# A two-block macaron layer on one core: the experts' results fetched in two parts, and several queues reordered

## The chip, the cores and the metric

One core of one Trainium2 chip runs the whole program. The metric is the device time of one execution in microseconds (us). Engines are named as in the profile: PE (TensorE), DVE (VectorE), ACT (ScalarE), POOL (GpSimd), SP (the engine that only issues DMAs here).

## The reference

`x` is (8, 256, 128) in float32, 2048 tokens of 128 numbers. Three steps follow one another:

```python
x = x + 0.5 * ffn(layernorm(x))     # first feed-forward block
x = x + attention(layernorm(x))     # 16 heads of 8 numbers, 256 keys, rotary embedding
x = x + 0.5 * ffn(layernorm(x))     # second feed-forward block, same weights

def ffn(x):
    shared = (silu(x @ sg.T) * (x @ su.T)) @ sd.T          # hidden size 256
    logits = x @ gate_w.T                                  # 8 experts
    top = argmax(logits); xs = x * sigmoid(max(logits))
    routed = (silu(xs @ wg[top].T) * (xs @ wu[top].T)) @ wd[top].T
    return shared + routed
```

## The kernel before, in words

The tokens lie in `x` as 16 tiles of 128 (a tile has one token on each partition); four tiles are a chunk, two tiles are a batch of attention. Every engine runs its own written-out queue, and semaphores order them. The work has five stages.

**First front** (`ffn(0)` up to `routed`). DVE takes moments of each chunk, POOL turns the variances into inverse deviations (`ffn_rstd`), DVE normalises, PE transposes (`turn_chunk`) and multiplies with the gate (`logits`). DVE chooses an expert for each token (`choose`), PE counts tokens by expert (`count`), DVE works out each token's slot (`place`). This is done in two steps: tiles 0 to 11 (`FIRST = 12`), then 12 to 15. ACT scales the tokens (`scale`), and POOL scatters them by slot into `xs_sorted` in DRAM, one indirect DMA a tile (L323). Between these, PE does the shared expert chunk by chunk: `shared_gate`, `shared_up`, `shared_down`; ACT applies SiLU (`silu`), DVE multiplies (`shared_hidden`) and adds to `x` (`shared_add`). `find_experts` tells PE which expert each slot tile has; PE loads these 23 numbers into registers.

**Routed experts** (`routed`). 23 slot tiles (`SLOT_TILES`) are loaded back (`LOADS`, on SP), and each goes through its expert: PE transposes, gate and up products, SiLU on ACT, product on DVE, transposes, down product. POOL scatters each result tile to its tokens' rows in `y_by_token` (L332). The scatter of tokens is such that the tokens of tiles 0 to 11 are all in slot tiles 0 to 18.

**Return.** SP waits for all 23 result scatters (`y_scattered`), then loads the results in four pieces of a chunk into `yg`, which lies in the same memory as `xs`. DVE adds half of them to `x` (`add_experts`, L782).

**Attention** (`attention(turn)`, turns i = -3 to 8). A turn has 16 steps n on each engine. PE computes scores of batch i twice: in one orientation for the row maxima (`scores`, DVE `maxima`, L801), which run 12 steps ahead, and in the other for the exponentials (`scores_t`, ACT `exponentials`, L535). Around them are the later batches' normalisation, projections (`project`), rotary embedding (`rope` on DVE, `rotate`, `remainder`, `third` on POOL, `first` and `second` on ACT), and the transposes `turn_parts` of queries and keys in halves (qa, ka, qb, kb) and of the halves with the maxima's parts in them (ma, mb). POOL's `split_max` makes these parts from the eight maxima of a half. The copies out of PSUM are `copy_queries` and `copy_keys`. Turns -3 to -1 are the prologue. The last two turns hold parts of the second block's front.

**Second front, routed experts, return** (`ffn(1)`): as before, then SP stores `x` to `out_x` in four pieces, each after its `add_experts`.

## Time and profile before

| | |
|---|---|
| Three runs | 351.35, 354.33 and 354.4 us, median 354.33 |
| The profiled execution | 352.44 us, of which the span from first to last instruction is 350.6 |
| Mean granted clock of PE | 0.953 |
| Busy shares | PE 82%, DVE 66%, ACT 57%, POOL 46% |
| The chain that ended last, by engine | PE 50%, DVE 27%, DMA 6%, issue 6%, POOL 5%, ACT 4% |
| Stages in the span | first front to 49.4, routed experts to about 89, return and prologue of attention to about 124, attention to about 270, second front to 297.8, routed experts to 337.5, return and stores to 350.6 |

Times within the span are microseconds from its start. The busy shares are averages over stages with different limits, so they are to be read by stage. The 1.84 us outside the span are start and end of the execution.

### The profile page before, as it was taken

To read this page: it belongs to the slowest core of one execution; us is meant where nothing else is said; L and a number is where in the kernel's file an instruction comes from. 1 tells how busy PE (TensorE), PEld (TensorE's weight loads), DVE (VectorE), ACT (ScalarE), POOL (GpSimd) and SP (SyncE) were. 2 spreads that over 40 slices of the span, in tenths; PEclk is the share of its full clock that TensorE was granted. 3 is DMA by queue.
4 is the path that set the end of the run, shared out by engine and by line. 5 is a ranking of instruction groups with operands and counts; after the bars stand their busy time and mean duration, and the time that the engine had idled before them with its cause. 6 is when DMAs were issued, how large, how long until landed. Compare 5 with 4: busy or idle time off the path is not lost.

```text
span 350.6 us, 6524 instructions
## 1 busy us (share of the span) xinstructions
PE 287.1 (82%) x2124; PEld 181.0 (52%) x2146; DVE 232.0 (66%) x633; ACT 198.6 (57%) x440; POOL 161.1 (46%) x295
## 2 busy tenths in 40 slices
PE   0799959999145579999999999998999897999940
PEld 0765536666013235565656555555485565566630
DVE  6648814343165988898989899997966686334323
ACT  1254215454214578989898989897857531455410
POOL 2405788766334635253535264541210675256550
PEclk9999999999755999999999999999998999999995
DMA  7992136111310000000000000000000013511118
GB/s 205 169 328 94 53 91 132 53 47 37 107 43 0 2 0 4 0 3 2 0 2 3 0 3 2 2 1 3 2 0 3 23 55 85 142 47 37 39 46 239
DMA packets 24272, 18.42 MB, mean 53 GB/s; under 512 B 4944, under 2 KB 22608, under 8 KB 23984
## 3 DMA queue, kind: packets, MB, share of 16 engines
q1 hardware_dynamic: 21744, 12.88, 14.9%
q0 software_dynamic: 2496, 5.13, 4.5%
q8 instruction: 18, 0.29, 0.4%
q14 instruction: 14, 0.11, 0.1%
HBM read 10.30 MB, written 7.71 MB: 51 GB/s over the span
## 4 chain that ended last, share of the span: by engine, by line
PE 50%; DVE 27%; DMA 6%; issue 6%; POOL 5%; ACT 4%; SPq 1%; POOLq 0%; another core or an unknown queue 0%; DVEq 0%; ACTq 0%
PE bank L931 40%; DVE negmax L801 11%; PE bank L1098 3%; DVE qT L794 3%; PE bank L1060 3%; DVE xn L612 2%; DMA xs<-y_by_token 2%; DVE rs L818 1%; PE bank L1046 1%; PE bank L940 1%; DMA y_by_token<-ys,xg 1%; DMA x<-in_x 1%; DVE stats L622 1%; ACT kT L542 1%; DVE sh L719 1%
## 5 line engine op out<-in xcount | busy, mean ns | idle before, releaser
L801 DVE TENSOR_REDUCE negmax<-bank 128x2 f32<-128x512 f32 x128 | 83.5, 682 | 5.7 <-PE bank L931 4.1
L535 ACT ACTIVATE probs<-bank 128x512 f32<-128x512 f32 x128 | 71.8, 603 | 16.2 <-PE bank L931 15.8
L332 POOL DMA_INDIRECT y_by_token<-ys,xg x46 | 44.7, 972 | 32.5 <-issue 22.9
L766 DVE TENSOR_TENSOR rh<-rsg,bank 128x256 f32<-128x256 f32 x46 | 19.4, 421 | 47.5 <-ACT rsg L513 47.5
L931 PE MATMUL bank<-qT,kT 128*128 128x256 bf16 x256 | 49.1, 276 | 1.7 <-ACT qT L551 0.7
L323 POOL DMA_INDIRECT xs_sorted<-xs,slot x32 | 32.2, 1006 | 39.5 <-ACT xs L467 16.4
L931 PE MATMUL bank<-rgu,xgT 128*128 x92 | 47.2, 596 | 0.7 <-ACT xgT L505 0.7
L931 PE MATMUL bank<-kT,qT 128*128 128x512 bf16 x106 | 40.3, 380 | 5.0 <-DVE negmax L801 3.6
L513 ACT ACTIVATE rsg<-bank 128x256 f32<-128x256 f32 x46 | 17.7, 385 | 36.9 <-PE bank L931 36.9
L931 PE MATMUL bank<-probs,vx 128*32 128x256 f32 x512 | 35.0, 393 | 0.0
L542 ACT COPY kT<-bank 64x1024 bf16<-64x1024 bf16 x32 | 32.1, 1004 | 5.0 <-PE bank L1098 4.2
L1098 PE MATMUL bank<-tabb,parts 128*128 128x128 bf16 x384 | 30.1, 223 | 4.4 <-POOL parts L365 2.2
L931 PE MATMUL bank<-xnT,shgu 128*128 128x512 f32 x64 | 32.3, 635 | 0.5 <-DVE x L869 0.5
L1098 PEld LDWEIGHTS bank<-tabb,parts 128*128 128x128 bf16 x384 | 24.9, 100 | 13.6 <-POOL parts L365 8.2
L931 PEld LDWEIGHTS bank<-qT,kT 128*128 128x128 bf16 x256 | 21.0, 98 | 18.7 <-issue 8.3
L376 POOL TENSOR_TENSOR rot<-rc,rs 128x256 f32<-128x256 f32 x16 | 11.6, 725 | 38.7 <-DVE rs L818 38.7
L931 PE MATMUL bank<-rdn,rhT 128*128 x184 | 28.3, 277 | 0.1
L563 ACT CAST parts<-rot 128x384 bf16<-128x384 f32 x32 | 14.7, 507 | 19.3 <-POOL rot L376 16.3
L931 PEld LDWEIGHTS bank<-rdn,rhT 128*128 128x128 f32 x184 | 24.2, 191 | 0.5 <-issue 0.5
L362 POOL CAST parts<-negmax 128x16 bf16<-128x16 f32 x16 | 4.2, 260 | 38.8 <-DVE negmax L801 38.8
L931 PEld LDWEIGHTS bank<-probs,vx 128*32 128x32 f32 x512 | 13.5, 110 | 15.9 <-issue 5.5
L505 ACT COPY xgT<-bank 128x128 f32<-128x128 f32 x46 | 11.8, 260 | 15.1 <-PE bank L1046 15.1
(114 smaller groups left out, 493.2 us busy)
## 6 DMA issues: line engine op xcount, KB each, us to landing
rgu<-in_rgu SPq DMA_DIRECT2D x1, 2048.0 KB, 20.1
xs<-y_by_token SPq DMA_DIRECT2D x8, 256.0 KB, 3.6
xg<-xs_sorted SPq DMA_DIRECT2D x6, 258.0 KB, 4.4
xs_sorted<-xg SPq DMA_DIRECT2D x1, 1483.5 KB, 16.2
x<-in_x SPq DMA_DIRECT2D x4, 256.0 KB, 4.8
rdn<-in_rdn SPq DMA_DIRECT2D x1, 1024.0 KB, 16.2
out_x<-x SPq DMA_DIRECT2D x4, 256.0 KB, 2.6
xg<-xs_sorted SPq DMA_DIRECT2D x4, 193.5 KB, 3.7
```

What stands on the lines that cost most here:

```text
L323: g.indirect_dma_start(xs_dram, bass.IndirectOffsetOnAxis(ap=slot[:, i:i + 1], axis=0), xs[:, i, :], None, bounds_check=SLOT_TILES * P - 1 ...
L332: g.indirect_dma_start(y_dram, bass.IndirectOffsetOnAxis(ap=xg[:, j, D:ROW].bitcast(U32), axis=0), ys[:, j, :], None, bounds_check=N + SLO ...
L376: g.tensor_tensor(rot[:, t, :], rc[:, t, :], rs[:, t, :], ALU.add).then_inc(rotated, 1)
L505: a.copy(xgT[:, j % 2, :], gT_bank[j % 2][:, 0:P]).then_inc(gT_copied, 1)
L513: a.activation(rsg[:, 1 - u, :], gu_bank[1 - u][:, 0:F], ACT.Silu).then_inc(rsilu, 1)
L535: a.activation(probs[:, h % 8, :], stbank[st_bank(i, h)][:], ACT.Exp, scale=float(DH) ** -0.5).then_inc(exp_done, 1)
L542: ins = a.copy(kT[v][64 * k:64 * k + 64, 4 * half:4 * half + 4, k, :], src[64 * k:64 * k + 64])
L563: ins = a.copy(dst, part_of.unsqueeze(2).to_broadcast([P, H, rows, DH]))
L766: v_.tensor_tensor(rh[:, 1 - u, :], rsg[:, 1 - u, :], gu_bank[1 - u][:, F:2 * F], ALU.mult).then_inc(rh_ready, 1)
L801: v_.tensor_reduce(negmax[:, w, t, h0 + 2 * pair:h0 + 2 * pair + 2], sbank[k % 2][:].rearrange("p (a s) -> p a s", a=2), AX.X, ALU.max, ne ...
L931: return t_.matmul(o_, l, r, start=start, stop=stop, **k)
L1098: ins = t_.transpose(to[:, at:at + P], parts[w][:, t, q, h:h + 2, :].rearrange("p a c -> p (a c)"), identb)
```

## The change

1. **Layout in DRAM.** `x_in`, `y_by_token` and `out_x` are held partition by partition (the row of token (p, i) is p*16 + i), so that a partition's part of a load or store is one run of 1 or 2 KB instead of runs of 512 B. What lies in on-chip memory is the same.
2. **Return in two parts.** The results of tiles 0 to 11 are fetched once slot tiles 0 to 18 are scattered (`HOME = 19`), the rest after the last. There are six pieces (`PIECES`): tiles 0-1, 2-3, 4-7, 8-11, 12-13, 14-15. In the first block pieces 0 and 1 are added in turn -3, the others one by one at n = 13 of turns -2 to 1. The stores of `out_x` have the same pieces. All of SP's loads of results stand ahead of its stores in its queue.
3. **Slot tiles.** The first load of slot tiles (0-4) is split into 0-1 and 2-4.
4. **Queues of the fronts.** `count(0)` goes between the two halves of `shared_gate(0)`, ahead of `turn_chunk(3)`. Up products go ahead of down products. In the second block, gate and up of chunk 0 move from n = 6 and 10 of turn 8 to n = 4 and 6, and the logits of chunks 0 to 2 from n = 8, 8, 9 of turn 7 to 8, 10, 11. `count(1, 0)` goes from n = 15 to 14.
5. **Prologue of attention.** POOL's `inverse_std` of turn -2 goes ahead of `rotate`. In turn -1 the second projection with its `rope` goes behind the first two scores, and the transposes and copies of qb, kb and ma go to n = 11, the keys' copies staying at n = 9 of ACT's queue.
6. **ACT.** The SiLU table is loaded by a dummy activation at the top of turn 8; four tiles are scaled ahead of the first SiLU of the first block.
7. **`find_experts`** has one multiplication over 1x552 less.

```diff
-LOADS = [(0, SURE), (SURE, 8), (8, 12), (12, 16), (16, 20), (20, SLOT_TILES)]
+LOADS = [(0, 2), (2, SURE), (SURE, 8), (8, 12), (12, 16), (16, 20), (20, SLOT_TILES)]
+HOME = FIRST + E - 1
+PIECES = [(0, 2), (2, 4), (4, 8), (8, FIRST), (FIRST, 14), (14, TILES)]
...
-            xv = x_in.rearrange("(c i p) d -> c p i d", p=P, i=CHUNK)
+            xv = x_in.rearrange("p (c i d) -> c p i d", i=CHUNK, d=D)
...
-                sp.wait_ge(y_scattered, 16 * SLOT_TILES * (n + 1))
-                yv = y_dram[0:N, :].rearrange("(c i p) d -> c p i d", p=P, i=CHUNK)
-                for c in range(CHUNKS):
-                    sp.dma_start(yg[:, c * CHUNK:(c + 1) * CHUNK, :], yv[c]).then_inc(y_loaded[c], 16)
-            ov = out.rearrange("(c i p) d -> c p i d", p=P, i=CHUNK)
-            for c in range(CHUNKS):
-
-                sp.wait_ge(ffn_added, TILES + (c + 1) * CHUNK)
-                sp.dma_start(ov[c], x[:, c * CHUNK:(c + 1) * CHUNK, :]).then_inc(out_stored, 16)
+                yv = y_dram[0:N, :].rearrange("(p i) d -> p i d", i=TILES)
+                for k, (i0, i1) in enumerate(PIECES):
+
+                    if i0 == 0:
+                        sp.wait_ge(y_scattered[0], 16 * HOME * (n + 1))
+                    if i0 == FIRST:
+                        sp.wait_ge(y_scattered[1], 16 * (SLOT_TILES - HOME) * (n + 1))
+                    sp.dma_start(yg[:, i0:i1, :], yv[:, i0:i1, :]).then_inc(y_loaded[k], 16)
+            ov = out.rearrange("p (i d) -> p i d", d=D)
+            for i0, i1 in PIECES:
+
+                sp.wait_ge(ffn_added, TILES + i1)
+                sp.dma_start(ov[:, i0:i1, :], x[:, i0:i1, :]).then_inc(out_stored, 16)
...
+                if i == -2:
+                    inverse_std()
                 if T.pr:
                     rotate(0)
...
-                if T.nx:
+                if T.nx and i != -2:
                     inverse_std()
...
                     tanh(n, 0)
+                    scale(n, 0, range(HELD))
                     silu(0)
                     copy_chunk(n, CHUNKS - 1)
-                    scale(n, 0, range(FIRST))
+                    scale(n, 0, range(HELD, FIRST))
...
-                    if n == 13 and T.m:
+                    if n == (10 if i == -1 else 13) and T.m:
                         copy_queries("ma")
...
                     if i == B and n == 0:
+                        a.activation(table_use[:, 2:3], neghalf[:, 0:1], ACT.Silu)
                         scale(1, 0, range(HELD))
...
                 if i == -3:
+
+                    add_experts(0, 0)
                     moments_of(3, v)
+                    add_experts(0, 1)
...
+                    if n == 13 and -2 <= i <= 1:
+
+                        add_experts(0, i + 4)
...
-                    if n == 3 and T.pr:
+                    if n == (5 if i == -1 else 3) and T.pr:
                         rope(1)
...
-                    if n == 7 and T.m:
+                    if n == (11 if i == -1 else 7) and T.m:
                         copy_queries("qb")
...
-                    shared_gate(n, 0)
+                    shared_gate(n, 0, [0])
+                    count(n, 0)
+                    shared_gate(n, 0, [1])
+                    shared_up(n, 0)
                     turn_chunk(n, 3)
-                    count(n, 0)
-                    shared_up(n, 0)
                     logits(n, 3)
                     shared_gate(n, 1)
+                    shared_up(n, 1)
                     shared_down(n, 0)
-                    shared_up(n, 1)
...
-                    if i == B - 1 and n == 8:
-                        logits(1, 0)
-                        logits(1, 1)
-                    if i == B - 1 and n == 9:
-                        logits(1, 2)
-                    if i == B - 1 and n == 15:
+                    if i == B - 1 and n in (8, 10, 11):
+                        logits(1, (8, 10, 11).index(n))
+                    if i == B - 1 and n == 14:
                         count(1, 0)
-                    if i == B and n == 6:
+                    if i == B and n == 4:
 
                         pe.wait_ge(exp_done, H * B)
                         shared_gate(1, 0)
-                    if i == B and n == 10:
+                    if i == B and n == 6:
                         pe.wait_ge(pv_copied, B)
                         shared_up(1, 0)
...
-                    if n == 3 and T.pr:
+                    if n == (1 if i == -1 else 3) and T.pr:
                         project(0)
...
-                    if n == 3 and T.pr:
+                    if n == (5 if i == -1 else 3) and T.pr:
                         project(1)
...
-                    if n == 7 and T.m:
+                    if n == (11 if i == -1 else 7) and T.m:
                         turn_parts("qb")
-                    if n == 8 and T.m:
+                    if n == (11 if i == -1 else 8) and T.m:
                         turn_parts("kb")
...
-                    if n == 14 and T.m:
+                    if n == (11 if i == -1 else 14) and T.m:
                         pe.wait_ge(m_split, 2 * (i + 1) + 1)
                         turn_parts("ma")
```

## Rows read from the trace of the kernel before

**Rows 1.** Windows: length, busy (count) by engine, PEclk, DMA share, GB/s.

```profile
...
100.00:110.00 10.00, 4.44 (x15) 2.32 (x16) 6.92 (x24) 3.19 (x8) 5.33 (x11) 0.50 0.00 0
...
280.00:300.00 20.00, 17.83 (x96) 11.73 (x95) 13.04 (x35) 4.79 (x13) 11.85 (x13) 1.00 0.32 86
...
```

**Rows 2.** Chain of work that ended last, first front: start, us.

```profile
...
43.28 2.29 DMA xs_sorted<-xs,slot
45.58 3.71 DMA xg<-xs_sorted
...
```

**Rows 3.** Timeline, first front: start, us, operation, [idle before, releaser].

```profile
...
7.10 0.88 DVE L622 BATCH_NORM_STATS2 stats<-x 128x6 f32<-128x128 f32 x4 [1.54 <-DMA x<-in_x]
...
18.27 3.76 PE L931 MATMUL bank<-xnT,shgu 128*128 128x512 f32 x4
...
19.91 0.21 DVE L654 CAST onehotb<-onehot 128x96 bf16<-128x96 f32 x1
...
22.68 1.13 PE L931 MATMUL bank<-onehotb,tabb 128*128 128x96 bf16 x13
...
23.84 0.43 DVE L675 TENSOR_TENSOR over<-bank,tab 128x256 f32<-128x256 f32 x1 [3.63 <-PE bank L931]
...
45.00 2.02 PE L931 MATMUL bank<-shdn,sh 128*128 128x128 f32 x16 [1.57 <-DVE sh L719]
...
49.43 0.41 PE L1046 MATMUL bank<-tab,xg 128*128 128x128 f32 x2 [2.41 <-DMA xg<-xs_sorted]
...
```

**Rows 4.** Windows of half a microsecond in the opening loads.

```profile
...
3.00:3.50 0.50, 0.00 (x0) 0.00 (x0) 0.50 (x1) 0.00 (x0) 0.00 (x0) 1.00 0.92 335
...
8.00:8.50 0.50, 0.00 (x0) 0.00 (x0) 0.49 (x5) 0.00 (x0) 0.02 (x1) 1.00 1.07 360
...
```

**Rows 5.** Timeline, 76 to 122: first boundary, prologue of attention.

```profile
...
84.92 0.97 POOL L332 DMA_INDIRECT y_by_token<-ys,xg  x1 [0.66 <-issue]
...
90.61 0.97 POOL L332 DMA_INDIRECT y_by_token<-ys,xg  x1 [0.30 <-issue]
...
95.77 0.69 DVE L782 SCALAR_TENSOR_TENSOR x<-xs,x 128x512 f32<-128x512 f32 x1 [6.67 <-DMA xs<-y_by_token]
...
105.34 0.71 POOL L407 TENSOR_TENSOR rstd<-rstd,neghalf 128x2 f32<-128x2 f32 x1
...
109.15 1.89 PE L1098 MATMUL bank<-tabb,parts 128*128 128x128 bf16 x16 [0.95 <-POOL parts L389]
...
113.15 0.91 PE L931 MATMUL bank<-wqkv,xnT 128*128 128x384 f32 x2 [0.54 <-ACT kT L542]
...
117.91 2.03 ACT L542 COPY kT<-bank 64x1024 bf16<-64x1024 bf16 x2 [1.22 <-PE bank L1098]
118.03 1.87 DVE L801 TENSOR_REDUCE negmax<-bank 128x2 f32<-128x512 f32 x3
...
```

**Rows 6.** Timeline, 119.8 to 142: the first maxima turned.

```profile
...
122.37 0.62 PE L1098 MATMUL bank<-tabb,parts 128*128 128x128 bf16 x8 [0.32 <-POOL parts L365]
...
```

**Rows 7.** Timeline of DVE alone, 141 to 160: steady attention.

```profile
...
146.25 0.43 DVE L816 TENSOR_TENSOR rc<-bank,tab 128x256 f32<-128x256 f32 x1 [1.00 <-PE bank L931]
...
```

**Rows 8.** Windows of 2 us in the last turns.

```profile
...
264.00:266.00 2.00, 2.00 (x17) 0.94 (x10) 0.98 (x4) 0.29 (x1) 0.00 (x0) 0.50 0.05 12
...
```

**Rows 9.** Timeline, 245 to 301: from attention to the second front.

```profile
...
272.90 1.28 ACT L477 ACT_TABLE_LOAD   x1
...
275.95 1.98 PE L931 MATMUL bank<-xnT,shgu 128*128 128x512 f32 x4 [0.52 <-DVE x L869]
...
```

**Rows 10.** The page: DMA issues, KB each, us to landing.

```profile
...
xs<-y_by_token SPq DMA_DIRECT2D x8, 256.0 KB, 3.6
...
out_x<-x SPq DMA_DIRECT2D x4, 256.0 KB, 2.6
...
```

**Rows 11.** Timeline, 331 to 351: the tail.

```profile
...
341.29 2.01 SPq L292 DMA_DIRECT2D xs<-y_by_token  x4
...
346.19 1.46 DVE L782 SCALAR_TENSOR_TENSOR x<-xs,x 128x512 f32<-128x512 f32 x2 [0.30 <-DMA xs<-y_by_token]
...
```

66 lines of the change are left out of this document (29 added, 37 removed).

## The prediction

> **What bounds the kernel now.** I read the windows first, to cut the span into stages, then the chain of waits within each, and the timeline at each border. In the first front PE works almost without pause up to its last down product at 45.00, which ends at 47.02; then it waits 2.41 us for the first slot tiles [rows 3]. That load hangs on the twelfth token scatter, which takes 2.29 us to land, and on the load's own 3.71 us [rows 2]. So two paths end 2.4 us apart: POOL's scatters last, PE's shared expert next. The routed stage is a steady turn on PE which the change leaves alone. At the first border all engines stop: the last result scatter is issued at 90.61 and DVE's first addition starts at 95.77, after 6.67 us idle [rows 5]. In the prologue that follows each engine waits for another, and PE is granted 0.50 of its clock, the 1.2 GHz level, with 4.44 us of work in 10 [rows 1]. From the first turned maxima, at 122.37 [rows 6], to about 270 attention is balanced: DVE, PE and ACT each work over nine tenths of the time. The second front is PE's: 17.83 of 20 us busy [rows 1]. In the tail nothing but DMA and four additions is left: the loads of results are issued from 341.29, the last addition ends at 347.65 [rows 11], and a store takes 2.6 us more [rows 10].
>
> **First front: 2.3 us (1.0 to 3.3).** The count of tiles 0 to 11 needs the one-hot table, ready at 20.12 (19.91 + 0.21), but runs at 22.68, behind the whole first gate product and a transposition; DVE's placing starts at 23.84 [rows 3]. Half a gate product (half of 3.76) fills PE until 20.15. The count then takes its 1.13, or up to 1.5 since early matmuls are slow (the gate's four take 3.76 here and 1.98 in the second front [rows 3, 9]), so placing starts near 21.6: 2.2 us earlier. The first load becomes two tiles instead of five, which I take as 0.9 of its 3.71. The scatter path thus gains 3 us and is no longer last. What is late next is PE: its 2.41 us of waiting are the most it can give, less what the new order costs it. Here the fourth chunk's transposition stands directly ahead of its logits, and PE must wait for ACT's copy between them, about 0.6 us; the wait for the hidden product that it had before the first down product (0.5 us) goes. The 1.57 us before the last down product [rows 3] stay, since PE loads the expert numbers there. With the slow matmuls shifted a little I get PE's end 0.6 later than 47.02, so 1.8 us gained by this edit. The removed multiplication in `find_experts` and ACT's four early scalings lie beside PE's work and count for nothing; if that cover went, they would cost 0.7 and 1.3.
>
> The new layout of `x` can move the start of everything: DVE waits 1.54 us for chunk 1 [rows 3], which is its bound. The nearest rows say how much longer runs bring: with 512 B runs alone on the queues the engines moved 335 GB/s at a share of 0.92, with weights in long runs 360 at 1.07 [rows 4]. The half megabyte ahead of and in chunk 1 would come 0.1 to 0.3 us sooner by that; fewer descriptors may also fill the dip between the first loads. I take 0.5 of 0 to 1.4. The Trainium skill (DMA: Bandwidth & Descriptors, Specifications) gives 512 B as the smallest transfer at line rate; by that rule the longer runs bring nothing and the front's sum would be 1.8. Rows 4 nearly agree.
>
> **First border and prologue: 4.5 us (3.0 to 6.5).** The nineteenth scatter is issued at 84.92 [rows 5]. Landing like those of [rows 2] it is home by 87.2; a load of results lands after 2.8 to 3.6 us [rows 10], so batch 0 is there at about 90.0, when DVE has just ended its last copy. POOL cannot take the variance before its last scatter is out, 90.61 + 0.97 = 91.6. Before, it began after the addition (0.69) and the moments (about 0.9), near 97.4. So the chain starts 5.7 us earlier. The POOL step moved ahead of `rotate` in turn -2 took 105.34 + 0.71 back to 105.03, 1.0 us between the second rotation and the remainder [rows 5]; ACT's part of that tile hides 0.2 of it, so 0.8 more: the first transposition of queries, 109.15 before, comes 6.5 earlier.
>
> Then turn -1 gives some of it back. The second projection (0.91 at 113.15 [rows 5]) behind two scores lets the maxima start 8 us earlier than before in all, but its `rope` (1.0) then stands among them. The eighth maximum ends 7.4 earlier, and so do the maxima's parts. But qb and kb are now transposed only after the eighth scores. The keys' two copies on ACT take 2.03 [rows 5] and start when kb is there; scores 9 wait for them, and DVE, which had those copies long done before, stands idle for 1.7 us (its queries' copy fills the rest). The addition of piece 3 (0.69, row of 95.77) and the `rope` also count. From first to thirteenth maximum DVE took 9.8 us; I get 9.8 + 1.0 + 1.7 + 0.7 = 13.2 (a maximum is 0.6, from three in 1.87 [rows 5]). So 8.0 - 3.4 = 4.6 at the top of turn 0. ACT's second parts stand behind the copy of ma; POOL's third parts end 2.6 us later against the maxima, and PE waits for them with the next queries: I get 5.6 gained there, so DVE's stream decides. The low end takes the queries' delay in full twice; the high end has the maxima's parts (7.4) decide less 0.9 for DVE.
>
> **Turns 0 and 1: -0.2 (0 to -0.8).** Two additions of half size, 0.4 each, enter DVE's steady stream. DVE idles 1.00 us a turn at its projections [rows 7], which hides most of them.
>
> **Turn 7: +1.0 (0 to 1.6).** PE is the bound here: 2.00 busy of 2.00, at granted 0.50 in 264 to 266 [rows 8], right behind a block of 24 logits products of 8 columns. Spread over n = 8, 10, 11 the logits no longer stand in a block, and I expect no fall; PE's roughly 3 us at half rate in and beside that window would come back as half of it, less what isn't PE's.
>
> **Turn 8: -0.4 (-1.0 to +0.3).** The gate product fills PE's 0.8 us wait for ACT's copy. But the SiLU table's 1.28 [rows 9], hidden nowhere before the first SiLU, now stands ahead of that copy, and up stands ahead of the back transposition of the outputs instead of behind: PE then waits for DVE's copy (0.4) before the output product, and 0.5 after it as before [rows 9]. I get gate(1) at 276.4 instead of 275.95. Earlier counting moves the scatters, not PE.
>
> **Second front: 0 (-0.5 to +0.5).** The products are the same and PE is the bound; the reordering of up and down moves waits which sum to 0.5 either way.
>
> **Tail: 2.5 us (1.5 to 3.3).** Three quarters of the results are loaded and added while the last four slot tiles run, since 19 tiles are scattered some 6 us before the end. After the last scatter lands (341.28) two small loads are issued, landing near 344.3; two additions of 0.4 end at 345.0; the last store lands 2.6 later, 347.6. Before it was 347.65 + 2.6 = 350.2. The first four stores wait in SP's queue behind those loads, so they are issued from 342.2 on, and 0.77 MB at about 300 GB/s end near 346.3, ahead of the last. The low end lets this transfer push the last store by 1 us. A second effect of the early loads, that they share engines with the last four scatters, is hidden as long as those land before 341.3; POOL's 0.30 us gaps between them say they are issue-bound.
>
> **The sum.** 2.3 + 4.5 - 0.2 + 1.0 - 0.4 + 0 + 2.5 = 9.7 us off the profiled 352.44 (span 350.6 and 1.84 around it): 342.7. The median of the runs shown, 354.33, is 1.9 above the profiled execution. I name 343.5, between 342.7 and the 344.6 that the same step gives from the median.
>
> **The rivals.** *The clock falls in turn 7 all the same* (chance 0.25): the +1.0 is lost, 344.5. The Trainium skill (TensorE: Matmul & The Clock Gate, Why this matters for your kernels) has the throughput drop after idle gaps of PE; in rows 8 PE was not idle, so by that rule the order of logits would change nothing here. *The prologue keeps its gain* (0.15): the maxima's stream catches up in turn 0, since DVE has pauses there, and 6.5 of it remain: 341.5. *The reordered prologue gives most of it back* (0.2): keys' copies and second parts are late, PE waits in turn 0 for queries and again for keys, each of 2 us; then the border brings 2, and 346. It speaks for this that the sum of new waits on ACT's queue is 3.3 us; against it, that DVE's stream holds them once only. *The parts don't come home early* (0.04): the first loads wait in SP's queue or collide with the scatters, so that both borders stand as before; then 350. *Slower* (0.04): PE's clock, at 0.50 in the prologue [rows 1], does not come back at its end, because PE now stands still there between the eighth scores and ma and again before the queries. A steady turn at that level costs 5 us or more on PE, which is busy nine tenths at 2.4 GHz; from the second such turn on the gain of 9.7 is gone, and with three it is 358. My own forecast holds 0.32.
>
> **How the numbers follow.** The bounds of the terms reach from 351 to 337 if all fall one way, which they won't; the first three cases with theirs give 339 to 349.5. About 1% (3.5 us) is what a measurement of this kernel can tell from no change. Slower by more holds 0.03, within 1% 0.06, and the rest is faster.
>
> **What would show it.** In the new profile the routed stage starts near 47; DVE idles under 1 us at the first border, and POOL's first variance stands at its last scatter plus 0.1. In turn -1 DVE stands still before the ninth maximum. PEclk has no half-speed slice at turn 7. The last store lands about 6.3 us after the last scatter. A first border that still has DVE idle for 5 us, or more than 177 us from that first addition to the end of attention (now 174, from 95.77 to about 270), would make the prediction wrong.

## The result and the profile after

The changed kernel took 343.97 us (median of four runs, 342.91 to 344.98) where the kernel before took 354.2 (351.35 to 354.4, four runs): the ratio is 0.973, with a 95% interval of 0.967 to 0.979. The profiled execution took 343.49 us, with a span of 341.6, 9.0 less than the 350.6 before. On a second chip, where both were profiled again, it was 344.40 against 354.22, a ratio of 0.973 (0.967 to 0.979).

The rows that answer to those of before stand here in the order of the stages. First the page's line of the span and the timeline of the first front (start and length in us, engine, line, operation, idle time before it and what ended that).

```profile
span 341.6 us, 6561 instructions
...
21.86 0.42 DVE L683 TENSOR_TENSOR over<-bank,tab 128x256 f32<-128x256 f32 x1 [1.11 <-PE bank L940]
...
43.50 2.02 PE L940 MATMUL bank<-shdn,sh 128*128 128x128 f32 x16 [0.88 <-DVE x L733]
...
46.69 0.41 PE L1056 MATMUL bank<-tab,xg 128*128 128x128 f32 x2 [1.16 <-DMA xg<-xs_sorted]
```

Placing starts at 21.86 instead of 23.84, the last down product at 43.50 instead of 45.00, and the routed stage at 46.69 instead of 49.43 [rows 3]. PE still waits for the slot tiles, 1.16 us instead of 2.41. Next the first border and the prologue.

```profile
84.43 7.85 SPq L296 DMA_DIRECT2D xs<-y_by_token  x6
...
87.05 0.42 DVE L789 SCALAR_TENSOR_TENSOR x<-xs,x 128x256 f32<-128x256 f32 x1 [0.69 <-DMA xs<-y_by_token]
...
87.86 0.97 POOL L336 DMA_INDIRECT y_by_token<-ys,xg  x1 [0.30 <-issue]
...
88.84 0.28 POOL L410 TENSOR_SCALAR rstd<-meanvar 128x2 f32<-128x2 f32 x1
...
100.12 1.89 PE L1108 MATMUL bank<-tabb,parts 128*128 128x128 bf16 x16 [2.01 <-POOL parts L393]
...
112.81 0.62 PE L1108 MATMUL bank<-tabb,parts 128*128 128x128 bf16 x8 [2.24 <-POOL parts L369]
...
113.68 1.29 DVE L807 TENSOR_REDUCE negmax<-bank 128x2 f32<-128x512 f32 x2 [1.63 <-PE bank L940]
```

SP's loads start before the last scatter, and DVE's first addition waits 0.69 us instead of 6.67 [rows 5]. POOL takes the variance 0.01 us after the end of its last scatter. The queries' transposition stands at 100.12 instead of 109.15 [rows 5], the first turned maxima at 112.81 instead of 122.37 [rows 6]. DVE stands still for 1.63 us before the ninth maximum. Then windows of 2 us: the end of the prologue, and turn 7.

```profile
112.00:114.00 2.00, 1.05 (x10) 0.56 (x10) 0.37 (x2) 1.17 (x2) 0.61 (x3) 0.96 0.00 0
114.00:116.00 2.00, 1.57 (x6) 0.93 (x6) 2.00 (x4) 1.70 (x5) 0.83 (x2) 0.50 0.00 0
...
118.00:120.00 2.00, 2.00 (x14) 1.49 (x13) 1.36 (x3) 0.75 (x2) 0.00 (x0) 0.50 0.00 0
```

```profile
256.00:258.00 2.00, 2.00 (x27) 1.39 (x27) 0.17 (x1) 0.61 (x2) 0.00 (x0) 1.00 0.00 0
...
264.00:266.00 2.00, 1.85 (x8) 0.81 (x8) 1.08 (x5) 2.00 (x7) 0.00 (x0) 1.00 0.00 0
```

The granted clock (the last number but two) is at 0.96 while PE does only 1.05 us of work in 2, and is 0.50, the 1.2 GHz level, for the next 6 us, when PE works again. In turn 7 it stays at 1.00, where before it was 0.50 [rows 8]. Last the tail.

```profile
329.35 6.39 SPq L296 DMA_DIRECT2D xs<-y_by_token  x6
...
332.04 1.05 POOL L336 DMA_INDIRECT y_by_token<-ys,xg  x1 [0.30 <-issue]
...
334.70 0.69 DVE L789 SCALAR_TENSOR_TENSOR x<-xs,x 128x512 f32<-128x512 f32 x1 [0.23 <-DMA xs<-y_by_token]
335.78 3.47 SPq L301 DMA_DIRECT2D out_x<-x  x6
337.39 0.43 DVE L789 SCALAR_TENSOR_TENSOR x<-xs,x 128x256 f32<-128x256 f32 x1 [1.99 <-DMA xs<-y_by_token]
338.46 0.43 DVE L789 SCALAR_TENSOR_TENSOR x<-xs,x 128x256 f32<-128x256 f32 x1 [0.65 <-DMA xs<-y_by_token]
```

Four of six additions are done by 335.4; the last ends at 338.89 instead of 347.65 [rows 11].

**The time by stage.** Five rows of a timeline cut each span: the first transposition of a slot tile, the last result scatter of the first block, the first transposition of queries, the end of the last value product, and the same first two of the second block. This is the table of every profiled execution that follows below (us):

```
                 first  routed  border to  attention to  second  routed  tail   span
                 front          queries    last values   front
before           49.43  41.18   18.54      160.73        28.00   41.16   11.56  350.6
after            46.69  41.17   12.26      163.23        27.55   41.14    9.56  341.6
before_again     48.00  42.51   18.63      161.68        28.03   41.15   11.80  351.8
after_again      46.39  41.18   12.27      163.68        27.49   41.14    9.65  341.8
up_down_old      46.02  41.18   12.26      163.29        27.56   41.15   10.64  342.1
logits_old       46.81  41.19   12.28      163.52        27.52   41.15   11.23  343.7
x_rows_512       62.38  41.19   12.26      164.32        36.89   41.56    9.80  368.4
busy_pe          62.86  41.22   12.26      162.96        35.20   41.15   10.15  365.8
one_return       63.75  41.16   17.40      163.97        36.88   41.15   12.69  377.0
one_return_2     64.16  41.68   17.45      163.83        36.88   41.47   12.73  378.2
count_late       65.50  41.31   12.26      164.48        36.91   41.55   10.09  372.1
plain_turn       63.69  42.15   12.26      162.42        35.14   41.15   10.89  367.7
plain_turn_2     64.23  41.15   12.25      162.97        35.21   41.15   10.44  367.4
best_try         62.52  41.29   12.27      161.50        35.12   41.15   10.05  363.9
```

Between the two kernels the differences are much the same on both chips where both were profiled: +2.75 and +2.94 us up to the last scatter, +6.28 and +6.36 at the border, -2.50 and -2.00 in attention, +0.45 and +0.54 in the second front, +2.00 and +2.15 in the tail. The last eight rows come from chips on which both fronts take longer; that is told under the experiments.

Two of these sums hold different things in the two pairs. In the second, 1.33 of the 2.94 us is the first routed stage, which takes 42.51 us in before_again: the granted clock is 0.50 there from 48.3 to 51.7 us, as it isn't in before or in either profile of the changed kernel. And attention comes apart when it is cut at the ends of the value products of each batch. The five batches from the third to the seventh together take 90.0 us in all fourteen profiles; the rest is this (us):

```
                 queries to end  second   last
                 of first batch  batch    batch
before           38.06           18.35    14.32
before_again     40.38           18.35    12.96
after            41.02           18.81    13.40
after_again      41.45           18.82    13.39
up_down_old      41.09           18.81    13.40
logits_old       41.73           18.82    12.96
x_rows_512       42.12           18.80    13.40
busy_pe          40.76           18.82    13.39
one_return       41.76           18.82    13.39
one_return_2     41.63           18.81    13.39
count_late       42.26           18.82    13.39
plain_turn       40.19           18.82    13.39
plain_turn_2     40.74           18.81    13.40
best_try         39.76           18.35    13.40
```

Between kernels with the same steps the second and the last column repeat to 0.02 us (but for the 14.32, which holds the half-speed window of [rows 8]), so small effects can be read from them. The first column moves by up to 2.3 us between two profiles of one kernel; before, with 38.06, has the clock at 0.50 for 20 us up to 113.0, and before_again, with 40.38, for 27 and then 3.

### The profile page after: what moved, and what is told of

The parts are those of the page before. It is cut to its first block, busy times and chain, and to the rows that moved or that the text cites. A ratio compares the mean times of both kernels' runs of the same rounds, so it can differ in the third digit from the quotient of the medians.

```text
span 341.6 us, 6561 instructions
## 1 busy us (share of the span) xinstructions
PE 288.2 (84%) x2146; PEld 181.1 (53%) x2146; DVE 231.0 (68%) x634; ACT 199.0 (58%) x441; POOL 161.8 (47%) x295
## 4 chain that ended last, share of the span: by engine, by line
PE 54%; DVE 23%; POOL 6%; issue 6%; DMA 5%; ACT 4%; SPq 1%; POOLq 0%; ACTq 0%; DVEq 0%
PE bank L940 43%; DVE negmax L807 10%; PE bank L1108 4%; PE bank L1070 3%; DVE qT L800 2%; DVE xn L620 2%; DVE rs L824 2%; PE bank L1056 1%; DMA x<-in_x 1%; PE bank L949 1%; DVE stats L630 1%; POOL parts L393 1%; ACT probs L542 1%; DMA xs<-y_by_token 1%; DMA xg<-xs_sorted 1%
## 5 line engine op out<-in xcount | busy, mean ns | idle before, releaser
L940 PE MATMUL bank<-kT,qT 128*128 128x512 bf16 x128 | 49.5, 389 | 4.6 <-DVE negmax L807 2.9
L940 PE MATMUL bank<-qT,kT 128*128 128x256 bf16 x256 | 49.8, 278 | 0.3 <-ACT probs L542 0.2
L327 POOL DMA_INDIRECT xs_sorted<-xs,slot x32 | 32.1, 1002 | 35.9 <-ACT xs L473 27.5
L520 ACT ACTIVATE rsg<-bank 128x256 f32<-128x256 f32 x46 | 17.7, 384 | 36.9 <-PE bank L940 36.9
L1108 PE MATMUL bank<-tabb,parts 128*128 128x128 bf16 x384 | 30.8, 227 | 7.3 <-POOL parts L369 4.2
L940 PE MATMUL bank<-probs,vx 128*32 128x256 f32 x512 | 34.0, 385 | 0.0
L940 PE MATMUL bank<-xnT,shgu 128*128 128x512 f32 x64 | 31.2, 621 | 1.0 <-DVE x L875 0.5
L940 PEld LDWEIGHTS bank<-kT,qT 128*128 128x128 bf16 x128 | 12.5, 99 | 13.4 <-DVE negmax L807 6.6
```

The costliest lines, as they stand in the source:

```text
L327: g.indirect_dma_start(xs_dram, bass.IndirectOffsetOnAxis(ap=slot[:, i:i + 1], axis=0), xs[:, i, :], None, bounds_check=SLOT_TILES * P - 1 ...
L520: a.activation(rsg[:, 1 - u, :], gu_bank[1 - u][:, 0:F], ACT.Silu).then_inc(rsilu, 1)
L940: return t_.matmul(o_, l, r, start=start, stop=stop, **k)
L1108: ins = t_.transpose(to[:, at:at + P], parts[w][:, t, q, h:h + 2, :].rearrange("p a c -> p (a c)"), identb)
```

## The experiments

The kernels ran in three batches, each on one chip. The kernel before took 370.65 us on the chip of the first batch, 354.22 on that of the second, 369.81 on that of the third. So every time here is read as a ratio to the kernel before on its own chip, and the table above stage by stage. Each edit is one to the changed kernel.

**The return in one part** (first and third batch).

```diff
                     if i0 == 0:
                         sp.wait_ge(y_scattered[0], 16 * HOME * (n + 1))
+                        sp.wait_ge(y_scattered[1], 16 * (SLOT_TILES - HOME) * (n + 1))
```

> The changed kernel, but SP waits for all 23 result scatters before the first piece; pieces and layout stay. Theory A, the early return is worth what the two borders moved: POOL's first variance goes from 88.84 to near 94 (+5), the tail loses its 2.0, the whole is 6 to 7.5 us slower, about 351. Rival B, at the first border the prologue's other waits absorb part of it: +3 to +4 there, the whole 5 us slower or less.

> The changed kernel with the whole return behind the last scatter again (its first load waits for all 23, nothing else is changed), on another chip than the first time. Theory: the split return is worth 6 to 7 us at the first border and 1.5 to 2 in the tail, and what the attention stage pays for the additions inside it does not come back, since they stay there: 7.5 to 9 us slower than the changed kernel, near 352.5 where the kernel before takes 354 (ratio 0.993 to 0.998). Rival: most of the border's gain comes from the reordered start of attention, so that without the split it still stands; then 348 or less.

Measured: 379.34 us, ratio 1.025 (1.021 to 1.029), and 379.43, ratio 1.024 (1.019 to 1.028). The nearest kernels with the split return have 0.998 to 1.001 on these chips, so the split is worth 2.4 to 2.6% of 370, 9 to 10 us: more than the 6 to 7.5 and the 7.5 to 9 expected, and both rivals fall (the prologue's other waits absorb part of it; the reorder carries the border). The absolute 352.5 couldn't be tested, since the chip was another. The timeline of the second run at the border:

```profile
105.84 0.97 POOL L337 DMA_INDIRECT y_by_token<-ys,xg  x1 [0.31 <-issue]
108.15 3.00 SPq L297 DMA_DIRECT2D xs<-y_by_token  x6
110.66 0.43 DVE L790 SCALAR_TENSOR_TENSOR x<-xs,x 128x256 f32<-128x256 f32 x1 [6.33 <-DMA xs<-y_by_token]
...
123.29 0.93 PE L1109 MATMUL bank<-tabb,parts 128*128 128x128 bf16 x7 [2.01 <-POOL parts L394]
```

(The last row is cut short by the end of its window.) DVE's wait of over 6 us is back. The stage from last scatter to queries is 17.40 and 17.45 us, against 12.26 with the split and 18.54 before: of the border's 6.3 us the split holds 5.2, and 1.1 stays without it, with POOL's reordered step and the smaller first pieces. The tail is 12.7 instead of about 10. The two stages make some 7.7 us; where the rest of the 9 to 10 is isn't settled. The second front takes either 35.2 or 36.9 us on these chips, and is in the longer form here. It is so in the four profiles that keep turn -1 as changed (these two, x_rows_512, count_late), and in the shorter form in the four with the old turn or with PE's stand in it filled. What joins the two places isn't known; the clock is at 0.50 for 10 us in the longer form and for 3 to 7 in the shorter.

**The order of turn -1** (first and third batch). Eight conditions go back to those of before:

```diff
-                    if n == (1 if i == -1 else 3) and T.pr:
+                    if n == 3 and T.pr:
                         project(0)
...
-                    if n == (11 if i == -1 else 7) and T.m:
+                    if n == 7 and T.m:
                         turn_parts("qb")
```

> The changed kernel with turn -1 ordered as before (second projection and rope at n = 3, qb, kb at n = 7 and 8, ma at n = 14 on PE and 13 on ACT). The first POOL step of turn -2 and the two-part return stay. Theory A, DVE's stream of maxima decides and the reordered turn -1 costs it time: thirteenth maximum 2 to 3 us earlier than in the changed kernel (117.69), the whole 1.5 to 2.5 us faster, about 342. Rival B, the earlier maxima's parts (ma) are what counts: without the reordering the attention starts later and the whole is 1 to 3 us slower, 345 to 347.

> The changed kernel with the order of turn -1 of before: second projection at n = 3, its queries and keys turned at n = 7 and 8, the mask at 14. Theory by the trace (a stand of 1.6 us before the ninth maximum, and keys' copies that scores 9 wait for): the reordered turn brings nothing, 344.4 within 0.8. My prediction took the reorder as part of what the border gains (maxima 1 us earlier) and of what it gives back (3.4); if the giving back is the reorder's, this one is 1 to 2 us faster. Rival: the old order makes the clock fall longer or holds the maxima back: 1 us or more slower.

Measured: 369.32 us, ratio 0.999 (0.995 to 1.002), and 369.16, ratio 0.999 (0.996 to 1.001). By time that is no different from x_rows_512 (0.998) and busy_pe (1.001), which keep the new order. By stage attention takes 162.42 and 162.97 us, against 163.83 to 164.48 in the four profiled kernels of those chips that keep it and have nothing added. So by the profiles the reorder takes some 1.4 us rather than bringing any. That is just under the 1.5 to 2.5 of the first expectation, and inside the 1 to 2 of the second's "if the giving back is the reorder's"; it is too small for the ratios to show. The table puts all of it before the end of the first batch's values.

**Work for PE after the keys' transposition** (first batch). Turn -1 gets eight products whose results nobody reads:

```diff
                         turn_parts("kb")
+                        if i == -1:
+                            for _ in range(8):
+                                mm(bank[4][:], qT[0][:, 0, 0:P], kT[0][:, 0, :, :].rearrange("p a s -> p (a s)"))
```

> The changed kernel with eight products of 128x128 by 128x512 (bf16, result unused, into a bank that is free then) on PE in turn -1 between kb and ma, where PE waits 2.2 us. Theory A, the granted clock fell from 1.00 to 0.50 from about 113.9 to 120.4 because PE had little to do before, and this cost about 1.2 us: with the added work the clock stays at 1.00 and the whole is 0.8 to 1.4 us faster. Rival B, the fall costs nothing on the deciding path, or the added work itself delays ma: 0 to 0.5 us slower.

Measured: 370.47 us, ratio 1.001 (0.998 to 1.004). The windows of the kernel with the eight products, and then those of x_rows_512, which has none and whose timeline stands within 0.6 us of it here:

```profile
126.00:128.00 2.00, 2.00 (x15) 1.30 (x15) 1.90 (x5) 0.00 (x0) 1.46 (x6) 0.54 0.03 8
128.00:130.00 2.00, 2.00 (x17) 1.05 (x15) 1.00 (x2) 1.58 (x2) 1.01 (x4) 1.00 0.00 0
130.00:132.00 2.00, 1.43 (x13) 0.79 (x12) 1.05 (x2) 1.85 (x4) 0.00 (x0) 1.00 0.00 0
132.00:134.00 2.00, 1.29 (x7) 0.37 (x5) 2.00 (x5) 1.42 (x4) 1.72 (x4) 1.00 0.00 0
```

```profile
128.00:130.00 2.00, 0.62 (x8) 0.46 (x9) 0.48 (x1) 1.96 (x3) 0.96 (x4) 1.00 0.00 0
130.00:132.00 2.00, 1.41 (x5) 0.74 (x6) 1.56 (x3) 2.00 (x5) 0.36 (x1) 0.68 0.00 0
132.00:134.00 2.00, 1.77 (x8) 0.59 (x6) 2.00 (x6) 0.78 (x2) 1.76 (x4) 0.50 0.00 0
134.00:136.00 2.00, 2.00 (x16) 1.60 (x15) 1.32 (x6) 0.60 (x1) 0.00 (x0) 0.50 0.00 0
```

With PE's stand filled (2.00 busy instead of 0.62 in the window before) the clock stays at 1.00, and attention takes 162.96 instead of 164.32 us. In every other profile of a kernel with the new order the clock is at 0.50 in windows behind this point, so the late fall goes with the stand; that is one profile against eight. Against the four of these on the same kind of chip attention is 0.9 to 1.5 us shorter. The mean granted clock of whole executions points the same way: 0.916 to 0.927 in the ten executions of busy_pe, against 0.907 to 0.914 in eight of the ten of x_rows_512. The times don't: the profiled execution is the fastest of its ten by 1.6 us, the median is no lower than that of x_rows_512 (370.47 and 370.32), and the 0.8 to 1.4 us expected for the whole are not to be seen. The shorter input rows of x_rows_512, worth 0.5 to 1.9 us to its first front, may hide a part of them. Nor does a kernel need the reorder to have such a fall: before_again and plain_turn_2, in the old order, have one as well, behind windows in which PE works 0.77 and 0.91 us in 2; before, plain_turn and best_try have none behind the prologue's.

**Input rows of 512 bytes again** (first batch).

```diff
-            xv = x_in.rearrange("p (c i d) -> c p i d", i=CHUNK, d=D)
+            xv = x_in.rearrange("(c i p) d -> c p i d", p=P, i=CHUNK)
```

> The changed kernel with the input x laid out and loaded as before, in runs of 512 B; results and output keep their layout. Theory A, the run length of x is worth nothing or costs: chunk 1 landed at 7.63 in the changed kernel against 7.10 before, so DVE's second moments start at 7.1 and the whole is 0 to 0.5 us faster. Rival B, those 0.5 us are chance of one execution and longer runs help by 0.3 to 0.5 us: second moments at 8 or later.

Measured: 370.32 us, ratio 0.998 (0.995 to 1.001). First its opening moments of DVE, then those of the changed kernel:

```profile
4.05 0.87 DVE L630 BATCH_NORM_STATS2 stats<-x 128x6 f32<-128x128 f32 x4
5.95 0.87 DVE L630 BATCH_NORM_STATS2 stats<-x 128x6 f32<-128x128 f32 x4 [0.39 <-DMA x<-in_x]
```

```profile
4.49 0.87 DVE L630 BATCH_NORM_STATS2 stats<-x 128x6 f32<-128x128 f32 x4 [0.47 <-DMA x<-in_x]
7.63 0.49 DVE L630 BATCH_NORM_STATS2 stats<-x 128x6 f32<-128x128 f32 x2 [1.64 <-DMA x<-in_x]
```

(The last row is cut short by the end of its window.) The first chunk is worked on at 4.05 in all four profiles with the short rows (this one, best_try and both of before), and at 4.30 to 4.59 in the ten with the long ones; the second at 5.95 to 7.10 against 6.96 to 7.99. The first front of this kernel is 0.5 to 1.9 us shorter than those of the kernels on its kind of chip that have the long rows and the early count. The long rows delay the opening; they don't speed it up. So theory A has the direction right, though the 7.1 that it named is 5.95 here. The delay goes on to placing in full: in the eleven changed kernels with the early count placing starts 14.21 to 14.23 us after the moments of the second chunk, whenever these are.

**The two kernels once more** (second batch).

> The kernel before, unchanged, profiled beside the runs that follow. In the first batch it took 370.65 us instead of 354.2, and the kernels with the change had a stretch of 16 to 17 us in the first front, and one of about 10 us in the second, in which TensorE's products ended late: vector additions and sigmoids of the shared expert waited 5 to 12 us for products whose rows end long before. Theory A: these stretches belong to the chip, and in this kernel they are shorter or stand once (its time was 16 us up where that of the changed ones was 25 us up). Then where the time is about 370 the turn of the first slot tile starts near 60 and not at 49.4; where it is about 354 the rows are those of the profile of before, within 0.5 us. Rival B: what grew is in the attention stage, and the fronts are as they were (turn at 49.4 at any time of the whole).

> The changed kernel, unchanged. Theory A (the late products in the fronts are a thing of that chip): ratio 0.973 (0.967 to 0.979) where the kernel before takes 354, with the turn of the first slot tile at 46.7; 0.995 to 1.00 where it takes 370, with the turn near 63. Rival B (the first batch's kernels were slow by their own edits): 0.973 at either time of the kernel before.

Measured: 353.56 us in one run, and 344.40 (343.68 to 345.65) with a ratio of 0.973 (0.967 to 0.979). The chip was one on which the kernel before takes 354, so A and B could not be parted by the times; 46.39 for the changed kernel is as expected (46.7), but 48.00 for the kernel before is 1.4 us short of the 49.4 that was to repeat within 0.5. What the second profile of the kernel before showed besides is a difference between two profiles of one kernel:

```profile
48.00 0.43 PE L1046 MATMUL bank<-tab,xg 128*128 128x128 f32 x2 [2.64 <-DMA xg<-xs_sorted]
```

```profile
124.00:126.00 2.00, 1.84 (x11) 1.15 (x11) 1.09 (x3) 0.97 (x1) 1.40 (x4) 0.50 0.00 0
...
262.00:264.00 2.00, 2.00 (x21) 1.99 (x19) 0.69 (x1) 0.94 (x2) 0.00 (x0) 1.00 0.00 0
264.00:266.00 2.00, 2.00 (x27) 1.59 (x29) 0.59 (x2) 0.99 (x2) 0.00 (x0) 1.00 0.00 0
```

In the window of [rows 8] the clock is at 1.00 here, in the same program, with PE just as full. And the late fall at the end of the prologue, which the changed kernel has, is there in the kernel before as well (0.50 at 124 to 126). Of the 1.4 us in the first front 0.7 is the second chunk of `x`, worked on at 6.41 instead of 7.10. The second front, the border and the second routed stage repeat within 0.1 us; the first routed stage takes 1.33 us more, with the clock at 0.50 for 3.4 us at its start.

**Logits in the steps of before** (second batch).

```diff
-                    if i == B - 1 and n in (8, 10, 11):
-                        logits(1, (8, 10, 11).index(n))
-                    if i == B - 1 and n == 14:
+                    if i == B - 1 and n == 8:
+                        logits(1, 0)
+                        logits(1, 1)
+                    if i == B - 1 and n == 9:
+                        logits(1, 2)
+                    if i == B - 1 and n == 15:
                         count(1, 0)
```

> The changed kernel with the logits of the second half taken in the steps of before (two thirds of them at turn 8 together, the last third at 9, the gate at 15 instead of 14). Theory: the packed 8-column products are what made TensorE's clock fall to 0.50 near the end of turn 7 in the kernel before, and it falls again here: 1.0 to 1.6 us slower than the changed kernel, with a half-speed window near 258 to 262. Rival: the fall hung on the state of the clock in the turns ahead, not on the logits: no half-speed window, and the time within 0.5 us of the changed kernel.

Measured: 343.4 to 345.5 us in four runs, ratio 0.969 (0.962 to 0.977). A fifth took 1581.84 us, for which nothing on record gives a reason; the ratio leaves it out. The packed products don't bring the clock down:

```profile
260.00:262.00 2.00, 1.93 (x28) 1.49 (x31) 0.95 (x5) 2.00 (x6) 0.00 (x0) 1.00 0.01 4
262.00:264.00 2.00, 2.00 (x33) 1.07 (x30) 1.86 (x8) 1.97 (x5) 0.00 (x0) 1.00 0.00 0
```

Attention takes 163.52 us, within 0.2 of the changed kernel's 163.68 on the same chip. The theory falls, the rival stands. The spread logits even cost a little: the last batch takes 12.96 us here and in before_again, and 13.39 or 13.40 in all eleven profiles with the new steps. In this attention most of the 0.43 us is offset by the first column, 0.28 longer than in after_again.

**Up products behind down products again** (second batch). In both fronts, on PE and DVE:

```diff
-                    shared_up(n, 1)
                     shared_down(n, 0)
+                    shared_up(n, 1)
                     count(n, 1)
                     shared_gate(n, 2)
+                    shared_down(n, 1)
```

> The changed kernel with one edit undone: the shared expert's up products again behind the down products of the tile before, on TensorE and on VectorE alike. My steps put the gain of the first front at 1.8 us for the order and the count together; the share of the up and down order is 0.5 to 1.3 us of it, and about 0.5 in the second front: 1 to 2 us slower than the changed kernel (ratio 0.976 to 0.979 where the kernel before takes 354). Rival: the gain is the count's alone, and this kernel is equal to the changed one within 0.5 us. Where the kernel before takes 370: if the late products come from the new order, which puts 128x512 products of three tiles close together, this kernel is 5 to 10 us faster than the changed one there.

Measured: 344.53 us, ratio 0.973 (0.967 to 0.979), the same as the changed kernel. The first front is 0.4 us shorter with the old order, which is as much as its second chunk of `x` came earlier (7.21 against 7.62), and the second 0.07 longer. The expected 1 to 2 us fail and the rival stands: the order of up and down is worth nothing here.

**The count behind the first gate product again** (third batch).

```diff
-                    shared_gate(n, 0, [0])
+                    shared_gate(n, 0)
                     count(n, 0)
-                    shared_gate(n, 0, [1])
```

> The changed kernel with the count of tiles 0 to 11 behind the whole first gate product again, and ahead of the fourth chunk's transposition as now. Theory: half a gate product (1.8 us) later placing moves the first slot tiles' load by the same; that path now ends with TensorE's own, so the routed stage starts 1.0 to 1.8 us later, 345.4 to 346.2. Rival: the front's gain came from the short first load (two tiles instead of five) and from taking the count ahead of the fourth transposition; then within 0.5 us of 344.4.

Measured: 372.64 us, ratio 1.007 (1.004 to 1.009), against 0.999 for plain_turn_2 on the same chip. The first front is 65.50 us, 1.3 to 2.6 longer than in the five profiles from these chips with the early count and the same long rows. Placing, which hangs on the count, is late by 1.3; first this kernel, then plain_turn_2:

```profile
23.55 0.42 DVE L683 TENSOR_TENSOR over<-bank,tab 128x256 f32<-128x256 f32 x1 [2.78 <-PE bank L940]
```

```profile
22.21 0.42 DVE L683 TENSOR_TENSOR over<-bank,tab 128x256 f32<-128x256 f32 x1 [1.12 <-PE bank L940]
```

From the moments of the second chunk it is 15.89 us instead of 14.22, so the edit moves placing by 1.67, near the 1.8 reckoned. What that is worth at the front's end is not shown. On this kind of chip the first slot tiles are loaded from 45.05 and turned at 65.50, so the load isn't what the front waits for, and its 1.3 to 2.6 us come another way. On the other kind the turn follows the load's issue by 3.1 us, and the shift would reach it almost whole; that is an estimate from the rows of the changed kernel, and count_late didn't run there. The larger gap of the whole times, 3.5 us, holds the second front's other form (36.91 against 35.21) and turn -1's order as well.

**Four edits together** (third batch): the order of turn -1 and the input rows as above, and two new ones.

```diff
-                    if n == 13 and -2 <= i <= 1:
+                    if n == (13 if i < 0 else 1) and -2 <= i <= 1:
                         add_experts(0, i + 4)
...
+            for i0, i1 in PIECES:
+                act.wait_ge(ffn_added, TILES + i1)
+                a.dma_start(ov[:, i0:i1, :], x[:, i0:i1, :]).then_inc(out_stored, 16)
```

(The second takes the stores out of SP's queue and puts them into ACT's.)

> Four edits on the changed kernel: the order of turn -1 of before, the input rows in 512 byte runs again, the additions of the last two pieces at n = 1 of turns 0 and 1 instead of n = 13, and the stores issued from ScalarE's queue, so that they don't stand behind the last two loads in SyncE's. Theory: the stores are out as each piece is added, which takes 0.5 to 1.0 us from the tail; the rest is worth 0 to 0.8 together: 343 to 344. Rival: the earlier stores collide with the last two loads, and the additions at n = 1 stand in front of the rotation: 344.4 or above.

Measured: 368.14 us, ratio 0.994 (0.991 to 0.996), against 0.999 for plain_turn_2 beside it: 1.0 us less by the medians, 1.8 by the ratios. It is faster than the kernel before there; the changed kernel didn't run beside it, and on a chip of the other kind it didn't run at all, so 343 to 344 stays untested. Attention takes 161.50 us, 1.2 less than with the old turn alone (162.42 and 162.97). Of this 0.46 is the place of the additions: the second batch takes 18.35 us instead of 18.82. The rest is in the first column, which differs as much between profiles of one kernel, and the profiled execution was the fastest of twelve, 2.5 us under the median. The tail:

```profile
353.85 1.08 POOL L331 DMA_INDIRECT y_by_token<-ys,xg  x1 [0.30 <-issue]
354.12 7.70 ACTq L610 DMA_DIRECT2D out_x<-x  x6
...
360.54 0.83 DVE L788 SCALAR_TENSOR_TENSOR x<-xs,x 128x256 f32<-128x256 f32 x2 [2.96 <-DMA xs<-y_by_token]
```

The stores start right away, but DVE now waits 2.96 us for the last loads, where plain_turn_2 had 1.87 and 0.38. The tail as a whole is 0.4 us shorter than there, but tails with nothing changed in them range from 9.56 to 11.23 us. What makes them differ is when the last scatter is home and the last two loads can go: 2.8 to 4.7 us after its start. From the issue of these loads to the end best_try takes 6.09 us, and the nine other profiles with the split return 6.47 to 6.75, so the earlier stores bring 0.4 to 0.7, in one profile.

**The two kinds of chip.** Where the kernel before takes 370 us, the kernels with the change have first fronts of 62 to 66 us instead of 46, and second fronts of 35 to 37 instead of 27.5; every other stage is nearly as on the other chips. Their timeline begins to differ near 32 us. These are rows of plain_turn:

```profile
35.28 1.95 PE L940 MATMUL bank<-shdn,sh 128*128 128x128 f32 x16
...
48.93 0.69 DVE L733 SCALAR_TENSOR_TENSOR x<-bank,x 128x512 f32<-128x512 f32 x1 [8.53 <-remote]
48.99 1.09 ACT L483 ACTIVATE sgate<-bank 128x512 f32<-128x512 f32 x2 [11.80 <-remote]
...
51.03 4.41 DVE L711 CAST expert<-expertf 1x23 int32<-1x23 f32 x1
...
53.58 1.83 POOL L348 MEMSET parts<- 128x2048 f32 x1
...
60.15 3.75 PE L940 MATMUL bank<-shdn,sh 128*128 128x128 f32 x16 [6.98 <-issue]
```

PE's down products of the second chunk are recorded as over at 37.23, yet DVE's addition, which needs them, is released at 48.93, and the profile finds no releaser ("remote"). Then the conversion of 23 expert numbers takes 4.41 us instead of 0.17, and PE, which loads these numbers, stands still for 6.98, of which 4.7 us are after the conversion has ended; nothing in the profile says what ends them. How much of this the kernel before has there isn't known, as no profile of it was taken on such a chip: its total is 16 us up, that of the changed kernels with the split return about 25. So on these chips the change without its split return loses 2.4% against before, by the ratio of one_return, and with it comes out even. The stages that the table shows longer are the two fronts, so the loss is most likely there; which of its edits brings it stays open. The early count is not it (count_late is slower still); the order of up and down wasn't tried on such a chip.

## Why the prediction was right

It named 343.5 us, and the median is 343.97. By its own terms, against the two pairs of profiles:

- **First front, 2.3: measured 2.75 and 2.94** (up to the last scatter). 1.33 of the 2.94 is the half-speed stretch of before_again behind the front, so the front itself gave 2.74 and 1.61. The first load was issued 2.00 and 0.61 us earlier, and the first transposition followed its issue after 3.1 us instead of 3.85 and 4.09 (the load itself took 2.98 us instead of 3.71 in the first pair, where 2.8 was reckoned). The count moved placing by 2.0 in the first pair, where 2.2 was reckoned, and by 0.3 in the second; count_late puts the edit at 1.67. The difference between the pairs is mostly the kernel before, whose second chunk came 0.7 us earlier the second time and whose gate products ran at half pace until 20.95 us instead of 24.23. The term for the longer input rows had the wrong sign: not +0.5, but -0.5 and -1.2 by the second chunk's moments (7.63 after 7.10, 7.62 after 6.41). The 512 byte rule, named there as the one by which longer runs bring nothing, was nearer, yet it too missed that they cost. PE's last down product, which was to end 1.8 us earlier, ended 1.5 earlier and, in the second pair, 1.2 later (45.36, then 46.53). And the scatter path, said to be last no longer, still is in the first pair, where PE waits 1.16 us for the load.
- **First border, up to the queries, 6.5: measured 6.28 and 6.36.** The two parts, 5.7 for the earlier pieces and 0.8 for POOL's reordered step, measure about 5.2 and 1.1 by one_return, though there the pieces are small as well.
- **From the queries to the last values: -2.0 for the prologue, -0.2 for the additions, +1.0 for the clock in turn 7, together -1.2. Measured -2.50 and -2.00.** By the columns of the second table the prologue with what follows to the end of the first batch is -2.96 and -1.07, the additions are -0.46 and -0.47, and the last batch is +0.92 and -0.43. The stand before the ninth maximum is as reckoned (1.63 of 1.7), but a reorder of turn -1 that costs 1.4 us by plain_turn was not needed for the border's gain. The step that failed is turn 7. I took a half-speed window of one profile for a thing of the program and gave its end to the spread logits; a second profile of the same kernel doesn't have it, and the old logits don't bring it. The +0.92 of the first pair belongs to that execution of the kernel before (14.32 us against 12.96 in the other), not to the change, and the spread logits cost 0.43. The rival about it, that the order of logits changes nothing, was right about the clock.
- **Turn 8 and second front, -0.4 and 0: measured +0.45 and +0.54 together.** The gate product came at 269.79, 6.16 us earlier against 6.53 at the end of turn 7, so turn 8 is -0.37 as said. The second front brought 0.8, where the waits of PE before its last down products shrank from 1.84 to 1.00. The up and down order isn't the cause, since up_down_old has 27.56; which edit is, was not tried.
- **Tail, 2.5: measured 2.00 and 2.15.** The last scatter is issued at 332.04, and the last two loads go out 2.82 us later (2.89 in after_again), where it was 2.25 in the kernel before and 2.30 in both profiles of one_return, which has no loads beside its last scatters. So the second effect that the prediction took as hidden, early loads sharing the engines with the last four scatters, is not: it costs 0.6 us here, and 0.8 to 2.5 in the eight other profiles with the split. The last addition then waits 1.99 and 0.65 us for its loads and ends 6.85 us after the last scatter's start, 0.9 later than reckoned; a store that took 0.4 longer in the kernel before than the 2.6 assumed gives some of it back.

The errors (+0.5, -0.2, -1.1, +0.9, -0.4, on the mean of the two pairs) nearly cancel, and within the first and the third term errors of both signs had cancelled already. The mechanism of the larger part, the return in two parts, is shown by one_return; the rest of the number was more luck than its terms deserve. The sign named for turn 7, no half-speed slice in PEclk, came true without the cause that it was to show.

Of the slower rival (the clock stays at 0.50 because PE stands still at the end of the prologue) the first half came true: the clock falls there for 6 us, and busy_pe, with the stand filled, doesn't have the fall and spends 0.9 to 1.5 us less in attention. But it comes back within turn 0, so the steady turns never ran at half speed. The Trainium skill (TensorE: Matmul & The Clock Gate, "HAM oscillation — how this bites in real kernels") says that a wait of PE between bursts makes the next burst start cold; these windows agree, 0.62 us of work in 2 ahead of a fall, and 2.00 ahead of none.

## What to carry to other kernels

Data that is needed in parts should be waited for in parts: one extra semaphore took 5.2 us from a border where every engine stood still, and about 2 from a tail, and no other edit of this change was shown to be worth half as much. A half-speed window in one profile isn't a property of the kernel until a second profile of it shows the same; where a term of a sum rests on one, take its chance as one in two. Loads started early share the engines with the transfers that the last loads wait for, so a part of what is won comes back as a later landing (0.6 us here, up to 2.5 in other kernels with the same loads). And a reorder that brings work closer together doesn't help when it leaves PE standing still at another place: fill the gap or leave the order.

## What the hardware showed that I had not expected

**Chips differ by more than the change.** The same two kernels give 354 and 344 on two chips. On two others the kernel before takes 370, and the nearest kernels to the changed one 370 as well. The fronts differ, by 16 to 18 and by 8 to 9 us; attention agrees within 1.3 us among the kernels with the new turn -1 and nothing added, the routed stages within 1.0.

**The clock's column says 1.00 where the trace has no record of the clock.** In the first front of the changed kernel two gate products of 512 columns take 2.06 us, and the four of the same kind at full pace in the second front 1.98:

```profile
18.80 2.06 PE L940 MATMUL bank<-xnT,shgu 128*128 128x512 f32 x2
```

```profile
18.00:20.00 2.00, 2.00 (x7) 1.28 (x7) 0.91 (x4) 0.21 (x1) 0.00 (x0) 1.00 1.02 274
```

That is the pace of the 1.2 GHz level under a printed 1.00. The trace's first record of the clock is a grant of 1.00 at 21.68 us, and the view prints 1.00 for what lies ahead of it as well. The second of the two products takes 1.06 us, and each of those from 22.18 on takes 0.59; in all fourteen profiles the products turn fast at their first record, which stands between 20.95 and 24.92. So here the records aren't wrong but begin late, and a front's early products are to be reckoned at half rate. The Trainium skill (TensorE: Matmul & The Clock Gate, "Seeing it yourself") warns that the clock's trace events have been seen to be unreliable on this chip; these rows don't show that.

**The clock fell once with PE full.** In the kernel before it goes to 0.50 at 263.2 us, after four windows of 2 us, from 254 to 262, with PE busy for 2.00 in each. In the thirteen other profiles, before_again among them, the clock stays at 1.00 in the same turn. It costs the last batch 1.36 us (14.32 against 12.96). No cause was found.

**POOL's memsets hold up a conversion on DVE.** In all eight profiles from the two slower chips the cast of 23 numbers starts among POOL's memsets, takes 4.29 to 5.82 us instead of 0.17, and ends 0.02 to 0.04 us after the last big memset (51.03 + 4.41 against 53.58 + 1.83 above). In the second front, with no memsets, it takes 0.17 there as well. The Trainium skill (SBUF — State Buffer, "SBUF: two separate sides") has the two engines share a pair of ports as an exclusive lock, held for a whole instruction. Here the cast waited through three memsets in a row, in count_late through four: it didn't get in between them. That the memsets are the cause is read from these coinciding ends; no run moved them.
